# Causal mask in an attention, GRU and expert kernel: one full-height matmul per head in place of four strip matmuls

## What is computed

```python
def _L0_attn_ref(x, wq, wk, wv, wo):          # D_MODEL 512, NHEAD 32, N_KV 8, HEAD_DIM 16
    q = bitlinear(x, wq).reshape(B, S, N_KV, G, HEAD_DIM)
    k = bitlinear(x, wk).reshape(B, S, N_KV, HEAD_DIM)
    v = bitlinear(x, wv).reshape(B, S, N_KV, HEAD_DIM)
    scores = jnp.einsum('bskgd,btkd->bkgst', q, k) * sm_scale
    causal = jnp.tril(jnp.ones((S, S), dtype=bool))
    scores = jnp.where(causal, scores, jnp.asarray(-jnp.inf, dtype=scores.dtype))
    probs = jax.nn.softmax(scores, axis=-1)
    out = jnp.einsum('bkgst,btkd->bskgd', probs, v)
    ...
    return bitlinear(out, wo)

x = x + _L0_attn_ref(_L0_cond_ref(x, cond_2048, 1, 1), ...)      # interpolation, then attention
x = x + _L0_ffn_ref(_L0_cond2_ref(cond_2048, x, ...), ...)       # GRU over 512 steps, then experts
```

## Time and profile before

| | us |
|---|---|
| median of 3 runs | 2597.84 (2595.99 to 2600.83) |
| the profiled execution | 2606.24 |
| its span in the profile | 2604.4 |
| attention, to about | 577 |
| granted TensorE clock, mean over the span | 0.975 |

### The profile page before, as it was taken

One profiled execution on the slowest core, in us unless ns is written; L12 is line 12 of the kernel. 1 busy time (PEld: TensorE's weight loads), 2 busy tenths in 40 slices (PEclk: granted clock), 3 DMA queues, 4 the chain that ended last, 5 costly groups with the idle time before them and its releaser, 6 DMA issues.

```text
span 2604.4 us, 143628 instructions
## 1 busy us (share of the span) xinstructions
PE 2127.1 (82%) x64092; PEld 1458.7 (56%) x64092; DVE 1663.7 (64%) x6182; ACT 1002.7 (38%) x3041; POOL 534.9 (21%) x1297
## 2 busy tenths in 40 slices
PE   6788888778888885477898984487898988989896
PEld 3334343446777774455666654465666666666564
DVE  5757565635666665677776767677676777767432
ACT  5464645353333332223343432223343443434342
POOL 2414021001111111112111413113112423113202
PEclk9899999899999999999999999999999999999998
DMA  4100000005011113001344542001344544444585
GB/s 166 53 19 18 19 2 3 2 27 187 31 33 37 44 39 104 4 4 36 121 162 139 159 146 77 4 20 54 117 157 153 157 134 126 144 142 155 191 288 199
DMA packets 109417, 239.41 MB, mean 92 GB/s; under 512 B 13952, under 2 KB 32896, under 8 KB 108672
## 3 DMA queue, kind: packets, MB, share of 16 engines
q1 hardware_dynamic: 96960, 182.25, 20.9%
q0 software_dynamic: 11840, 47.98, 5.9%
HBM read 170.93 MB, written 59.24 MB: 88 GB/s over the span
## 4 chain that ended last, share of the span: by engine, by line
PE 40%; DVE 25%; issue 8%; ACT 3%; DVEq 1%; DMA 0%; POOL 0%; POOLq 0%; ACTq 0%
PE ps L1566 23%; PE ps L1593 9%; DVE turn L1413 4%; DVE npre L1416 4%; PE ps L1630 4%; DVE turn L1407 3%; ACT parts_h L1303 3%; DVE hst L1424 3%; DVE turn L1402 3%; PE ps L1609 3%; DVE hst L1427 2%; DVE ur L1405 2%; DVE hnew L1425 2%; PE ps L1647 1%; DVE uz L1409 1%
## 5 line engine op out<-in xcount | busy, mean ns | idle before, releaser
L1566 PE MATMUL ps<-whh,hst 128*8 128x128 f16 x49152 | 826.9, 221 | 338.8 <-DVE hst L1427 260.5
L1566 PEld LDWEIGHTS ps<-whh,hst 128*8 128x8 f16 x49152 | 699.7, 88 | 536.4 <-DVE hst L1427 424.7
L1197 POOL COPY hb<-hst 128x32 f16<-128x32 f16 x512 | 174.3, 340 | 1404.9 <-DVE hst L1427 1404.8
L1296 ACT ACTIVATE keep_r<-ur 128x16 f32<-128x16 f32 x512 | 118.2, 231 | 808.4 <-DVE ur L1405 794.9
L1402 DVE STREAM_TRANSPOSE turn<-ps 128x128 f32<-128x128 f32 x512 | 162.6, 318 | 241.4 <-PE ps L1566 236.2
L1593 PE MATMUL ps<-bulk,xT 128*128 128x352 bf16 x1472 | 252.3, 314 | 2.8 <-issue 1.6
L529 DVE TENSOR_REDUCE mx<-ps 128x2 f32<-128x256 f32 (+3 forms) x256 | 196.4, 818 | 37.1 <-PE ps L717 36.7
L1424 DVE TENSOR_TENSOR_SCAN hst<-keep_z,parts_h 128x32 f16<-128x32 f32 x512 | 115.3, 225 | 160.6 <-ACT parts_h L1303 159.8
L434 ACT ACTIVATE stage<-ps,cs 128x1024 f32<-128x1024 f32 (+3 forms) x256 | 186.5, 790 | 73.3 <-PE ps L740 64.8
L1630 PE MATMUL ps<-bulk,hid 128*128 128x512 bf16 x744 | 205.5, 382 | 2.3 <-issue 1.2
L1407 DVE STREAM_TRANSPOSE turn<-ps 128x128 f32<-128x128 f32 x512 | 158.8, 310 | 45.3 <-PE ps L1566 43.7
(11 more groups left out here) (194 smaller groups left out, 2868.3 us busy)
## 6 DMA issues: line engine op xcount, KB each, us to landing
bulk<-in_experts SPq DMA_DIRECT2D x144, 352.0 KB, 4.9
bulk<-in_experts SPq DMA_DIRECT2D x72, 384.0 KB, 4.3
taken<-rows_in SPq DMA_DIRECT2D x92, 256.0 KB
rows_out<-yt SPq DMA_DIRECT2D x92, 256.0 KB, 2.2
rows_in<-taken SPq DMA_DIRECT2D x50, 256.0 KB, 3.3
gi_scratch<-bulk SPq DMA_DIRECT2D x72, 128.0 KB, 1.7
spare<-gi_scratch SPq DMA_DIRECT2D x36, 128.0 KB
gi<-gi_scratch SPq DMA_DIRECT2D x36, 128.0 KB
```

The source lines that it names most:

```text
L1566: mm = pe.matmul(ps[j * COLS:j * COLS + 2 * B, bank, 0:P], hst[:, 1 + 2 * B * k:1 + 2 * B * (k + 1)], whh[:, s, k, at:at + P], start=(k + ...
```

## The change

The mask is one 128 x 128 float16 matrix for each pass (-32768 above or below the diagonal, 0 elsewhere). It is added by one matmul per head: the moving operand is this matrix over all 128 rows, the weights are the 128 x 128 identity that the kernel already has. It still goes into the head's own bank and always covers the 128 columns of the diagonal block. 4 matmuls and 4 weight loads stand for 16 and 16. In the score pass `s_full` comes with heads 1 and 3 as before, but heads 0 and 1 are now complete before the masks of heads 2 and 3 have begun. One constant of 64 KB is loaded in place of two of 128 and 256 KB.

```diff
-        negR = sb("negR", [P, 4, P], F16)
-        maskR = sb("maskR", [P, 2, 4, P], F16)
+        mask = sb("mask", [P, 2, P], F16)
...
-                for c in range(4):
-                    for j in range(4):
-                        r = slice(32 * j, 32 * j + 32)
-                        mm = pe.matmul(ps[:, bank_of(n, j), st * P + 32 * c:(st + 1) * P], negR[r, c], maskR[r, 0, c, 32 * c:P],
-                                       start=False, stop=(c == 3), skip_group_check=True)
-                        if c == 3 and j % 2:
-                            mm.then_inc(s_full, 1)
+                for j in range(4):
+                    mm = pe.matmul(ps[:, bank_of(n, j), st * P:(st + 1) * P], ident[:], mask[:, 0], start=False, stop=True,
+                                   skip_group_check=True)
+                    if j % 2:
+                        mm.then_inc(s_full, 1)
...
-                for c in range(4):
-                    for j in range(4):
-                        r = slice(32 * j, 32 * j + 32)
-                        mm = pe.matmul(ps[:, bank_of(n, j), tt * P:tt * P + 32 * c + 32], negR[r, c], maskR[r, 1, c, 0:32 * c + 32],
-                                       start=False, stop=(c == 3), skip_group_check=True)
-                        if c == 3 and j % 2:
-                            mm.then_inc(s_full, 1)
+                for j in range(4):
+                    mm = pe.matmul(ps[:, bank_of(n, j), tt * P:(tt + 1) * P], ident[:], mask[:, 1], start=False, stop=True,
+                                   skip_group_check=True)
+                    if j % 2:
+                        mm.then_inc(s_full, 1)
...
-        "negR": (-HALF * np.eye(P))[rows32].astype(np.float16),
-        "maskR": np.stack([(r > rows32[:, :, None]), (r < rows32[:, :, None])], axis=1).astype(np.float16),
+        "mask": (-HALF * np.stack([r[None, :] > r[:, None], r[None, :] < r[:, None]], axis=1)).astype(np.float16),
```

More of the change, by code:

```diff
@@ L178, in _ @@
             sp.dma_start(st_wq, a["wq"].rearrange("p k n -> p (k n)")).then_inc(wq_in, 16)
-            for dst, src in ((negR, a["negR"]), (maskR, a["maskR"]), (sel, a["sel"]), (ident, a["ident"]), (bias, a["bias"])):
+            for dst, src in ((mask, a["mask"]), (sel, a["sel"]), (ident, a["ident"]), (bias, a["bias"])):
                 sp.dma_start(dst[:], src).then_inc(const_in, 16)
@@ L520, in _ @@
                 q_split(0, n)
-            dve.wait_ge(const_in, 5 * 16)
+            dve.wait_ge(const_in, 4 * 16)
             nc.vector.tensor_tensor(bias[:, 0, 0:2 * KT], bias[:, 0, 0:2 * KT], bias[:, 1, 0:2 * KT], ALU.add).then_inc(bias_ready, 1)
@@ L757, in _ @@
                     pass
-            pe.wait_ge(const_in, 5 * 16)
+            pe.wait_ge(const_in, 4 * 16)
             for b in range(B):
@@ L1733 @@
     sel = np.repeat((r[:, None] % 32 == 4 * np.arange(QT) + r[:, None] // 32)[:, :, None], P, axis=2).astype(np.float16)
-    rows32 = 32 * np.arange(4) + r[:, None] % 32
     cst = np.zeros((P, 8), np.float32)
```

## The result

The changed kernel takes 2618.1 us (median of 4 runs, 2614.92 to 2621.82) against 2599.34 us for the kernel before (now 4 runs): ratio 1.0077, 95% interval 1.0059 to 1.0094, so 15 to 24 us slower. The forecast was 2613.5 us, +15.7, in a range of 2604 to 2620; 2618.1 lies near the range's upper end. The profiled execution took 2621.82 us, with a span of 2620.0.

A forecast was written before the change was run, and what follows sets the result against it. Bound: in both attention passes VectorE and ScalarE wait for the end of TensorE's mask. Score pass 7.1 us plus head pass 8.6 us gives +15.7 us on 2597.8, so 2613.5 us; range 2604 to 2620.

The forecast's parts named there:

- the ring: Score pass: maximum, scores, mask, next maximum wait in a loop; head pass: TensorE and ScalarE wait for each other.
- (b): TensorE's change between strips of 32 rows and full-height matmuls: 0.09 us each way, 0.11 or 0.12 as upper end.
- (c): Four full-height mask matmuls of 128 columns stream in 0.224 us, 0.056 each, their weight loads running beside them.
- (d): Head pass, step from full-height mask to `heads_out` on 32 array columns: taken at 0.09 us, lower end nothing.
- First `s_full` at +0.06: Heads 0 and 1 complete 0.365 us after the strips' end, before 0.31: +0.06 us latency for a group.
- The term that was mis-sized: Head pass: 0.27 us more for each period of four groups, 32 periods, 8.6 us in sum.
- the slack of 0.12 us: Head pass, block 3: TensorE ready at 278.58, before scores at 278.70, so 0.12 us absorbs all but 0.03 of +0.15.
- 1, weight loads set the pace: Rival: the four identity loads do not overlap, four masks take 0.39 us; 23 us more, 2637 us; chance 0.05.
- 2, the change-over costs the mask nothing: Rival: the identity could be loaded before the strips end, so no change-over is paid; -3.4 us, 2594.4 us; chance 0.09.
- 3, the clock: Rival: half-clock stretches of the attention go, five of ten giving -15 us, 2598.5 us; chance 0.07.
- the prediction's own sign: What would show the clock rival in the changed profile: more than one half-clock stretch gone.
- The stop of 2.12 us: One stop put down to neither engine nor data; may go or stay, 0 to -2.1 us, taken at 0.

The follow-up runs named there:

- the kernel with 32 columns: Changed kernel with its mask matmuls cut to 32 of 128 columns and a mask of zeros, which masks nothing: ratio 0.9988 to the kernel before.
- the staircase mask: Kernel before, mask kept in 32-row strips as one rank-32 bfloat16 product per head, 4 matmuls for 16: 2567.15 us against 2589.78, ratio 0.9917.

## Why the prediction was right

**What bounds it**: right. The groups that wait longer, VectorE's and ScalarE's, wait for the mask (L714, L735; 4.1 and 5.6 us more, forecast 5 and 8), and the kernels with one pass changed show the ring in each pass by itself.

**The units.** (b), change-over 0.09: right. (c), four full masks in 0.224 us: nearly, 0.23 to 0.24, since a spacing is 0.060 in the mean and not 0.056. (d), full to 32 columns of the array: 0.09, right; the lower end, nothing, is out. First `s_full` at +0.06: the score period where only latency counts grew by 0.16 for 3 x 0.06. The Trainium skill's rule in TensorEngine Tiling (Array Packing), Key Properties, is that a change of tiling mode drains the engine. All of these traces agree with it as far as each change costs time, 0.09 us, and the kernel with 32 columns shows that apart from the columns; that it is a drain which takes this time, no run shows.

**The term that was mis-sized** is the head pass, 11.4 us where the sum had 8.6, on two points of block 3 and block 2. TensorE's own time for a group went up by 0.17 to 0.18, not 0.15, because of the spacing and the step to `heads_out`. And the slack of 0.12 us ahead of the scores at 278.70 was read too wide: from `heads_out` to the next scores TensorE takes 0.58 us by itself (283.21 to 283.79), not 0.52, so the slack was 0.06 and block 3 lost 0.12 in place of 0.06. Score pass: 7.8 for 7.1, the same spacing.

**What made up for it** was not in the sum: fewer and other half-clock stretches. In the attention the two first traces differ by 13 us, all of them by 15.5 in the mean. Both program ratios, 15 to 24 and 9 to 20 us, hold the forecast of 15.7, and also the 19.2 of the periods, so the time can't tell the two. That the profiled execution took 2621.82 us where the sum gave 2621.9 is luck: 12.9 us of its growth lie in the attention and 2.6 behind it, where the prediction had none and where the same instructions scatter by 17 us.

**The rivals.** 1, weight loads set the pace: out, four masks last 0.40 us. 2, the change-over costs the mask nothing: out, by the 0.44 us from scores to mask and by the mask of 32 columns. 3, the clock: by the prediction's own sign, more than one stretch gone, it did move. Of ten stretches (up to the one just behind the attention) eight are left in each of the three traces with the full mask, while the four with strips have nine or ten. It moved by a few us in favour of the change and not by enough to hide the loss; how much of it is the mask's doing stays open, as said above. The stop of 2.12 us did not come back at that place in the changed kernel: before it the second period of batch 0 took 8.95 us, afterwards 7.02; but one of the strips' three later traces (8.40, 6.77, 6.76) has something like it and two don't, so it can't be put down to the number of instructions.

## What to carry to other kernels

A small matmul of 32 rows that stands among others of its kind should stay there: going to full height costs a change-over of 0.09 us and gives up the four heads side by side, so a quarter of the instructions took 0.08 us longer in a group of the score pass and 0.17 to 0.18 in one of the head pass. Count streamed columns and changes of form before the number of instructions, but count that too where matmuls are narrow: 4 matmuls in place of 16 were worth 12 of the 20 us that the staircase mask gained. Where a constant only has to be "very negative or nearly zero", look for one of low rank in a type with a wide exponent. When a loop repeats, measure its period in the trace: it showed to 0.01 us a period what the program's time could show only to some 5 us. But such a sum leaves out the starts of the passes and the clock: here the traces of the attention had 15.5 of its 19.2 us.

## What was not expected of the hardware

- 0.09 to 0.10 us is the price of every change of form on TensorE that was looked at: strips to full, full to strips, strips to 32 columns and full to 32 columns.
- Sixteen strip matmuls of 32 columns cost 0.04 to 0.06 us more a group than four of 128, for the same columns (0.14 to 0.22 a period).
- The same pass of the changed kernel began at full clock, and at half clock after a shift of 1.7 us far ahead of it (its own start moved by 1.0 us), worth 1.7 to 2.0 us for each of two passes. The kernel before differed by 1.4 us at one of these places between two traces without any shift.
- Behind the attention, the same instructions took between 2032 and 2049 us in these traces, as much as the change itself moved; its cause is open.
